# The ramp of the first feed-forward reordered: first unit's norm first, weights scaled in two parts, filler products on TensorE

## The reference

```python
x = x + 0.5 * ffn(layernorm(x))
x = x + attn(layernorm(x), Q, K, VO)      # 16 heads, rank 64
x = x + 0.5 * ffn(layernorm(x))

def ffn(x):                                # three blocks
    h = x
    for blk in range(3):
        y = qlora_linear(h, 2*blk)         # w = (q/7.5 - 1)*scale, + bias, + lora_b @ lora_a
        y = gelu(layernorm(y) * gamma + beta)
        h = qlora_linear(y, 2*blk+1) + h
    return h
```

## Time and profile before

| | us |
|---|---|
| median of 3 runs | 995.24 (993.47 to 997.75) |
| profiled execution: its own time | 993.64 |
| profiled execution: span, first to last instruction | 991.8 |
| TensorE busy | 956.4 (96%) |
| VectorE busy | 853.0 (86%) |
| ScalarE busy | 809.2 (82%) |
| GpSimd busy | 831.7 (84%) |

### The profile page before, as it was taken

How to read it: one execution, slowest core, us unless ns; L and a number is a source line. 1 busy time by engine, 2 the same in 40 slices (tenths; PEclk the granted TensorE clock), 3 DMA queues, 4 the chain that set the end, 5 groups by cost and what they waited for, 6 DMA issues and landing times.

```text
span 991.8 us, 19434 instructions
## 1 busy us (share of the span) xinstructions
PE 956.4 (96%) x6005; PEld 509.0 (51%) x6005; DVE 853.0 (86%) x1731; ACT 809.2 (82%) x1344; POOL 831.7 (84%) x940
## 2 busy tenths in 40 slices
PE   4889799999999999999999999999999999999898
PEld 4677344444444444444444444444444444445677
DVE  7678899999999999999999999999999988995554
ACT  3876689888888898888888888888888888888773
POOL 3655599999998999899999999999999998899552
PEclk9999999999999999999999999999999999999999
DMA  9000322222222222222222222222222222220002
GB/s 252 1 2 11 86 65 64 65 64 65 64 62 58 64 64 56 67 63 62 61 61 63 65 64 65 64 65 64 64 65 64 65 64 55 69 62 10 1 1 86
DMA packets 71744, 59.89 MB, mean 60 GB/s; under 512 B 11168, under 2 KB 70560, under 8 KB 71648
## 3 DMA queue, kind: packets, MB, share of 16 engines
q1 hardware_dynamic: 71392, 58.31, 23.3%
q10 hardware_dynamic: 256, 0.39, 0.1%
HBM read 6.23 MB, written 2.10 MB: 8 GB/s over the span
## 4 chain that ended last, share of the span: by engine, by line
PE 90%; DVE 5%; POOL 2%; issue 1%; DMA 1%; ACT 1%; SPq 0%; POOLq 0%; DVEq 0%; ACTq 0%
PE ps L1194 12%; PE ps L1186 11%; PE ps L1196 11%; PE ps L1195 11%; PE ps L1187 11%; PE ps L1179 7%; PE ps L1170 3%; PE ps L1213 3%; PE ps L1209 3%; PE ps L1210 3%; PE ps L1092 3%; PE ps L1172 3%; PE ps L1171 3%; PE ps L1121 2%; PE ps L1102 1%; PE ps L1133 1%
## 5 line engine op out<-in xcount | busy, mean ns | idle before, releaser
L469 POOL TENSOR_TENSOR p_lo<-work_b,p_hi 128x1024 f16<-128x1024 f32 x256 | 540.0, 2131 | 48.2 <-ACT p_hi L620 47.6
L923 DVE TENSOR_REDUCE mcol<-ps 128x2 f16<-128x1024 f32 x256 | 301.2, 1221 | 3.5 <-PE ps L1179 3.4
L615 ACT ACTIVATE work_b<-ps,exp_scale 128x1024 f32<-128x1024 f32 x256 | 271.5, 1111 | 35.2 <-PE ps L1187 34.6
L620 ACT ACTIVATE p_hi<-work_b 128x1024 f16<-128x1024 f32 x256 | 256.1, 1055 | 0.0
L1194 PE MATMUL ps<-p_hi,xn_hi 128*128 128x512 f16 x512 | 194.7, 380 | 1.2 <-DVE pair_ops L912 1.2
L1186 PE MATMUL ps<-head_ops 128*128 128x512 f16 x512 | 194.1, 379 | 1.8 <-DVE head_ops L934 1.4
L1195 PE MATMUL ps<-p_hi,xn_lo 128*128 128x512 f16 x512 | 194.0, 379 | 0.0
L1196 PE MATMUL ps<-p_lo,xn_hi 128*128 128x512 f16 x512 | 194.0, 379 | 0.0
L1187 PE MATMUL ps<-head_ops 128*128 128x512 f16 x512 | 194.0, 379 | 0.0
L478 POOL TENSOR_TENSOR x<-x,o_sb 128x512 f32<-128x512 f32 x128 | 162.8, 1272 | 7.5 <-DVE o_sb L951 2.1
L934 DVE STREAM_TRANSPOSE head_ops<-mcol 32x128 f16<-32x128 f16 x512 | 155.4, 304 | 9.3
(11 more groups left out here) (135 smaller groups left out, 1375.2 us busy)
## 6 DMA issues: line engine op xcount, KB each, us to landing
head_ops<-pair_ops SPq DMA_DIRECT2D x512, 64.0 KB, 2.0
head_ops<-pair_ops SPq DMA_DIRECT2D x128, 128.0 KB, 2.4
x<-x_dram SPq DMA_DIRECT2D x8, 256.0 KB, 5.9
out<-x SPq DMA_DIRECT2D x8, 256.0 KB, 2.3
vo_last<-wvo_dram SPq DMA_DIRECT2D x1, 1024.0 KB, 12.2
qk<-wq_dram SPq DMA_DIRECT2D x1, 512.0 KB, 5.3
qk<-wk_dram SPq DMA_DIRECT2D x1, 512.0 KB, 6.1
scl<-scales_dram ACTq DMA_DIRECT2D x8, 48.0 KB, 5.0
```

What stands on the lines that cost most here:

```text
L469: pool.tensor_tensor(p_lo[:, k % 2, rows, :], p32[:, k % 2, rows, :], p_hi[:, k % 2, rows, :], ALU.subtract).then_inc(plo_done, 1)
L615: nc.scalar.activation(p32[:, k % 2, 2 * a:2 * a + 2, :], s_ps[a], ACT.Exp, scale=exp_scale[:, 0:1]).then_inc(exp_done, 1)
L620: nc.scalar.activation(p_hi[:, k % 2, 2 * a:2 * a + 2, :], p32[:, k % 2, 2 * a:2 * a + 2, :], ACT.Copy).then_inc(phi_done, 1)
L923: nc.vector.tensor_reduce(mcol[:, pair % 2, :, t, 0], max_ps[pair == 1][t % 2], AX.X, ALU.max, negate=True).then_inc(max_red, 1)
```

## The change

Four things in the first feed-forward's ramp; the second feed-forward and attention keep their order.

1. The norm is done unit by unit: batches 0 and 1, then 2 and 3, then 4 to 7 (three rounds of the 1/sigma chain). ScalarE makes batch 2's sums itself (`input_sums`). VectorE normalizes batches 0, 2, 4, 6, 7, ScalarE 1, 3, 5. VectorE does unit 0's seed, and z_scaled(0, 0), between the statistics.
2. Weights 0 and 1 are loaded and made first; weights 2 to 5 are dequantized and scaled by POOL (`scale_weights`) into `w_rest`, their LoRA part is copied by ScalarE, and VectorE adds and centres them in step 3 (`w_ready`, on which TensorE waits in step 4).
3. TensorE issues filler products (`keep_warm(10)`) twice; turns and products go unit by unit, and lin2(0, 0) stands ahead of pre(2).
4. POOL's clears of `head_ops` for the fourth operand go into steps 4 to 6; the load of ScalarE's Gelu table moves to the start.

```diff
 @block.sync
             for b in range(SG):
                 load_x(b)
-            sp.dma_start(qw[:, :, :], qw_d).then_inc(w_in, 16)
...
+            for g in range(G // 2, G):
+                load_scales(sp, g, slice(0, 2), w_first_in)
             for b in range(SG, B):
                 load_x(b)
+            sp.dma_start(qw[:, 2:NL, :], qw_d[:, 2:NL, :]).then_inc(w_rest_in, 16)
+            for g in range(G):
+                load_scales(sp, g, slice(2, NL), w_rest_in)
+            sp.dma_start(gam[:, :], gam_d).then_inc(gb_in, 16)
+            sp.dma_start(bet[:, :], bet_d).then_inc(gb_in, 16)
 @block.gpsimd
-            pool.wait_ge(prep_p, 5)
-            pool.memset(head_ops[64:128, :, 3, :], 0.0).then_inc(prep_p, 1)
-            pool.wait_ge(prep_p, 6)
-            pool.memset(head_ops[64:65, 0:2, 3, :], 1.0).then_inc(prep_p, 1)
-            pool.memset(head_ops[64:65, 2:RING, 3, :], 1.0).then_inc(prep_p, 1)
...
+            def scale_weights(dst, layers):
+                plink(pool, pool.tensor_scalar(dst, qw[:, layers, :], 1.0 / 7.5, -1.0, ALU.mult, ALU.add))
+                return pool.tensor_tensor(dst, dst, scl[:, layers, :], ALU.mult)
+
+            def clear_heads(part):
+                pool.wait_ge(rstd_ready, part + 5)
+                if part == 0:
+                    pool.memset(head_ops[64:128, :, 3, :], 0.0).then_inc(prep_p, 1)
+                else:
+                    pool.memset(head_ops[64:65, 2 * part - 2:2 * part, 3, :], 1.0).then_inc(prep_p, 1)
+                pool.wait_ge(prep_p, 6 + part)
+
+            pool.wait_ge(prep_p, 5)
             for i in range(STEPS):
                 newton(0, i)
                 if i == 0:
+                    pool.wait_ge(w_rest_in, 16 * (G + 1))
+                    scale_weights(w_rest[:, :, :], slice(2, NL)).then_inc(rest_scaled, 1)
                     pool.wait_ge(a_in, 16 * 4)
                 if i < H // 4:
                     fold_last(4 * i)
                     fold_last(4 * i + 2)
+                if i in (4, 5, 6):
+                    clear_heads(i - 4)
 @block.scalar
+            act.dma_start(bias[:, :], bias_d).then_inc(bias_in, 16)
+            act.dma_start(la[:, :, :], la_d).then_inc(lora_in, 16)
+            act.dma_start(lb[:, :, :], lb_d).then_inc(lora_in, 16)
+            act.dma_start(qw[:, 0:2, :], qw_d[:, 0:2, :]).then_inc(w_first_in, 16)
+            for g in range(G // 2):
+                load_scales(act, g, slice(0, 2), w_first_in)
             act.wait_ge(consts, 2)
+            nc.scalar.activation(gelu_warm[:, :], mean_mat[:, 0:1], ACT.Gelu)
...
+            def input_sums(b):
+
+                act.wait_ge(x_in[b], 16)
+                for t in range(TT):
+                    cols = slice(t * D, (t + 1) * D)
+                    ins = nc.scalar.activation(work_b[:, b, cols], x[:, b * TT + t, :], ACT.Identity, scale=1.0 / D,
+                                               accum_out=mv[:, b * TT + t, 0:1])
+                ins.then_inc(sums_done, 1)
+                act.wait_ge(sums_done, 1)
+                for t in range(TT):
+                    cols = slice(t * D, (t + 1) * D)
+                    ins = nc.scalar.activation(work_b[:, b, cols], x[:, b * TT + t, :], ACT.Square, scale=-1.0,
+                                               bias=mv[:, b * TT + t, 0:1], accum_out=mv[:, b * TT + t, 1:2])
+                ins.then_inc(sums_done, 1)
+
+            input_sums(2)
+            act.wait_ge(prep_pe, 2)
+            nc.scalar.activation(wt[:, 2:NL, :].rearrange("p n d -> p (n d)"), lora_rest, ACT.Copy).then_inc(lora_copied, 1)
...
+            act.wait_ge(moments_ready, 1)
+            norm_apply(1)
+            pre(0)
+            pre(1)
+            squares(0, 0)
+            act.wait_ge(moments_ready, 2)
+            norm_apply(3)
+            pre(2)
+            pre(3)
+            squares(0, 1)
+            act.wait_ge(moments_ready, 3)
+            norm_apply(5)
+            act.wait_ge(gb_in, 32)
+            gelu(0, 0)
+            pre(4)
+            pre(5)
+            squares(0, 2)
+            pre(6)
+            pre(7)
+            squares(0, 3)
+            for i in range(4, STEPS):
+                gelu(0, i - 3)
                 squares(0, i)
-                if i == 1:
-                    norm_apply(1)
-                    pre(1)
                 weight_halves(i)
 @block.vector
+            input_stats([0])
+            split_bias()
+            input_stats([1])
+            norm_means(batch_tiles(0, 2))
+            norm_sigmas(batch_tiles(0, 2))
+            norm_apply(batch_tiles(0))
+            dve.wait_ge(w_first_in, 16 * (G + 1))
+            link(dve, nc.vector.tensor_scalar(wt[:, 0:2, :], qw[:, 0:2, :], 1.0 / 7.5, -1.0, ALU.mult, ALU.add))
+            link(dve, nc.vector.tensor_tensor(wt[:, 0:2, :], wt[:, 0:2, :], scl[:, 0:2, :], ALU.mult))
             dve.wait_ge(prep_pe, 1)
...
+            centre(0, 1).then_inc(prep_v, 1)
+            input_stats([3])
+            norm_means(batch_tiles(3))
+            dve.wait_ge(sums_done, 2)
+            norm_sigmas(batch_tiles(2, 2), batch_tiles(2))
...
-            norm_input(1)
-            for i in range(STEPS):
+            seed(0, 0)
+            norm_apply(batch_tiles(2))
+            input_stats([4, 5, 6])
+            z_scaled(0, 0)
+            input_stats([7])
+            seed(0, 1)
+            norm_means(batch_tiles(SG, SG))
+            norm_sigmas(batch_tiles(SG, SG))
+            norm_apply(batch_tiles(4))
+            norm_apply(batch_tiles(6))
+            norm_apply(batch_tiles(7))
+            for i in range(2, STEPS):
+                if i == 3:
+                    dve.wait_ge(rest_scaled, 1)
+                    dve.wait_ge(lora_copied, 1)
+                    link(dve, nc.vector.tensor_tensor(wt[:, 2:NL, :], wt[:, 2:NL, :], w_rest[:, :, :], ALU.add))
+                    centre(2, NL).then_inc(w_ready, 1)
 @block.tensor
+            nc.tensor.matmul(bmean_ps, mean_mat[:, :], bias[:, :], start=True, stop=True).then_inc(bmean_done, 1)
...
+            def keep_warm(count):
+
+                for n in range(count):
+                    nc.tensor.matmul(warm_ps, mean_mat[:, :], mean_mat[:, :], start=True, stop=True)
+
+            keep_warm(10)
...
             pre(0)
-            turn_bias()
             pe.wait_ge(prep_v, 1)
             pe.wait_ge(bias_ready, 1)
-            for i in range(STEPS):
+            lin1(0, 0)
+            keep_warm(10)
+            pre(1)
+            lin1(0, 1)
+            turn_z(0, 0)
+            lin2(0, 0)
+            pre(2)
+            lin1(0, 2)
+            pre(3)
+            lin1(0, 3)
+            turn_z(0, 1)
+            for i in range(4, STEPS):
+                if i == 4:
+                    pe.wait_ge(w_ready, 1)
                 lin1(0, i)
-                if i == 1:
-                    pre(1)
...
```

More of the change, by code:

```diff
@@ L287, in at, with load_scales @@
             return (f * STEPS + i) * 2 + c + 1
+        def load_scales(eng, g, layers, done):
+            rows = 128 // G
+            eng.dma_start(scl[rows * g:rows * g + rows, layers, :],
+                          sc_d[g][layers, :].partition_broadcast(rows)).then_inc(done, 16)
         class Link:
@@ L528, in apply_half, with norm_apply @@
                 ins.then_inc(done, 1)
[L530 to L537, removed]
+            def norm_apply(b):
+                for t in range(b * TT, (b + 1) * TT):
+                    ins = nc.scalar.activation(xhat[:, t, :], x[:, t, :], ACT.Identity, scale=rstd[:, t:t + 1],
+                                               bias=shift[:, t:t + 1])
+                ins.then_inc(xhat_a, 1)
             def squares(f, i):
@@ L714, in _, with rsqrt @@
             link = Link()
-            def rsqrt(tiles):
+            def rsqrt(tiles, summed):
                 v, y, r, u = var[:, tiles], rstd[:, tiles], rs_t[:, tiles], rs_u[:, tiles]
-                link(dve, nc.vector.tensor_scalar(v, mv[:, tiles, 1], LN_EPS, None, ALU.add))
+                if summed is not None:
+                    nc.vector.tensor_scalar(var[:, summed], mv[:, summed, 1], 1.0 / D, LN_EPS, ALU.mult, ALU.add)
+                    plain = slice(summed.stop, tiles.stop)
+                else:
+                    plain = tiles
+                link(dve, nc.vector.tensor_scalar(var[:, plain], mv[:, plain, 1], LN_EPS, None, ALU.add))
                 link(dve, nc.vector.tensor_scalar(y.bitcast(I32), v.bitcast(I32), -0.5, MAGIC, ALU.mult, ALU.add))
@@ L818, in _, with input_stats @@
-            link(dve, nc.vector.tensor_reduce(wmean[:, :], wt[:, :, :], AX.X, ALU.add))
-            link(dve, nc.vector.tensor_scalar(wmean[:, :], wmean[:, :], -1.0 / D, None, ALU.mult))
-            for n in range(0, NL, 2):
-                ins = nc.vector.tensor_scalar(wt[:, n, :], wt[:, n, :], wmean[:, n:n + 1], None, ALU.add)
-            ins.then_inc(prep_v, 1)
+            def input_stats(batches):
+                for b in batches:
```

(11 more changed lines are left out.)

145 lines of the change are left out of this document (63 added, 82 removed).

## The result

The changed kernel takes 1002.15 us (median of 6, 1001.55 to 1004.33) against 995.37 (median of 6) of the kernel before: ratio 1.0073, 95% interval 1.006 to 1.0086. It is slower by 6.8 us. The forecast was 998.9, 4.5 above its base. A second measurement of the same kernel, described with the experiments, gave 1.0061 (1.0044 to 1.0079).

The account below looks back on a forecast made before the run. TensorE, busy 96% of the span, bounds the kernel, so the date it passes turn_tops decides. Later turn_tops +1.4 and slow pace +3.1 give +4.5 on a base of 994.4: 998.9 us, range 993.5 to 1002.5.

Parts of the forecast that it names:

- The middle, where the gain goes: Ramp from prep_v to turn_tops: moments_ready 3 1.1 later, TensorE standing 7.0 us, lin1(0,4) 2.3 later, turn_tops 1.4 later.
- B: TensorE at the gap ahead of lin2(0,0): pace stays fast, +1.4, 995.8 us; chance 0.24.
- D: Start on TensorE: filler products do not bring the pace, +9, 1003 us or more; chance 0.07.
- E: Norm of units 2 and 3 is not last; the start's 5.6 us carry through, less caps: -4, 990.4; chance 0.06.
- rival C: As forecast, but input_sums, first weights' loads slip and slow pace fills lin1(0,2): +6.5 to +7, 1001; chance 0.18.
- Costs nothing: POOL's clears moved into steps 4 to 6: newton(0,5) ends at 57.5, its z needed at 64.1; no cost.
- Slow pace, coming back within lin1(0,2): TensorE after standing 7.0 us: lin2(0,0), turns and part of lin1(0,2) at slow pace, +3.1.
- Nobody waits for it: keep_warm(10) fillers on TensorE: done between 12.3 and 14.5, no delay, as batch 1's xhat comes at 13.8.
- 1.4 forecast without the pace: Ramp's end at turn_tops: 57.0 against 55.57, counting order and waits without slow pace.

Follow-up runs that it names:

- VectorE's order: Changed kernel with norm_apply(2) and batch 4's stats ahead of seed(0,0), postponed weights and weight_maxima(0) ahead of seed(0,2) on VectorE: 997.54 us, 1.0024.
- the norm first: Combined-edits kernel (991.92 us) with batches 4 to 7's norm ahead of seed(0,1) and z_scaled(0,0), turn_z(0,0), lin2(0,0) and gelu(0,0) later: 990.6 us, 0.995.
- the moves at turn_tops: Changed kernel with weight_maxima(2) ahead of z_scaled(0,4) and turn_tops behind lin2(0,3): 1001.55 us, 1.0068.
- all edits together: Changed kernel with 30 fillers in the gap, clears at the start, folds later, maximum and turn_tops moved; lin2(0,0) stays ahead of unit 2: 997.35 us, 1.0027.

## Why the prediction was right or wrong

Right: the direction, and the mechanism up to lin2(0,0) and its slow pace. "The middle, where the gain goes" holds in each step: the start came 5.3 sooner (5.6 forecast), seed(0,0) at 18.52 (18.0), TensorE stood 7.7 us (7.0) ahead of lin2(0,0), released by Gelu behind norm_apply(5), and came out of it at half pace. lin1(0,4) followed 5.8 after the start of seed(0,2) (5.5 forecast). Rivals B, D and E are out: the pace fell, the fillers brought it (1.05 for the first eight, without them 1.91), nothing carried through. The measured 1002.15 lies at the upper edge of the range, where rival C stood, but not by C's mechanism: input_sums took 2.9 us, less than the 3.9 taken, no load of the first weights was late, and the pace was back before lin1(0,2).

Wrong: the size, 6.8 against 4.5, and with it the weight of the chances: I gave 0.66 to a change of under 0.5% and 0.30 to a slower kernel, and it is 0.7% slower. Three terms of the sum failed.

"Costs nothing" for the moved clears, and nothing for the folds. I followed POOL's work for when its results are needed, and not for what lies beside it on VectorE. POOL's first fold waited for vo_last until 28.25 (27 forecast), which put it beside the third chain. The folds cost 1.0 there (4.73 against 3.78 with the folds moved), and half a microsecond on L876 (0.98 for two at 45.20 beside a fold, 0.48 in the kernel of VectorE's order), the clear 0.75 ahead of turn_tops (2.37 against 1.63 with the clears moved). The Trainium skill, "SBUF — State Buffer", in the section on who interferes with whom, says that VectorE and GpSimd share a pair of ports which is locked for a whole instruction, and that the loser waits in full. By that rule a small instruction ends when POOL's does, and the traces agree (29.69 with 29.66, 59.15 with 59.12).

"Slow pace, coming back within lin1(0,2)" was taken as one stretch worth 3.1. It was worth less, 2.2 (11.49 against 9.32), as the pace came back during the turns of batches 4 and 5. But there were three stretches, 5.4 together; that the first was taken too dear hides 0.9 of the miss. The second follows 2.0 us of standing ahead of lin1(0,4) in six of the eight profiles that have this gap; it costs 1.65 in the profile after (lin1(0,4) to lin2(0,1) in 3.85 instead of 2.2). The third, behind turn_tops, costs 1.55 (4.25 against 2.70) in one profile of the changed kernel and nothing in the other. I had bounded the cost of standing by the gap of 2.57 in the kernel before, which kept its pace, and so held gaps of 2 us free. The same trace has the 2.45 us at 929.43, also without a fall; both were draws, as the other profiles show. The rule weighed in the prediction (the Trainium skill, "TensorE: Matmul & The Clock Gate", its part on the clock gate: an idle stretch brings the throttled state back) agrees with the first stretch, granted clock 0.50 from 32 to 34, and I didn't ask it about the shorter gaps. The row of 2.57 is one case, no bound: 2.0 us were followed by half pace here, 3.22 us in the kernel without fillers were not.

The dates ahead of the third chain were late: lin1(0,0) by 0.3, seed(0,0) by 0.5, seed(0,1) by 0.6. "Nobody waits for it" of the fillers was wrong: they ended at 13.55, both batches of unit 0 were normalized at 13.12, and their turns began only behind the fillers; in other profiles these ended up to 0.6 later.

The sum of the corrected terms, against the profile: 1.4 forecast without the pace, +0.5, +1.0 and +0.75 for the dates and POOL, 2.2 + 1.65 + 1.55 for the pace: 9.05 of 9.2, with differences of 0.3 either way left in the middle.

The medians are 6.8 apart because the profile before is a low draw, and because stretches of half pace come in some executions and not in others. Every timed execution comes with its span and mean granted clock. Of 65 executions of the kernel before, measured beside the experiments, 14 have a clock of 1.00 and spans of 991.6 to 992.8, 34 have 0.996 to 0.998 (991.6 to 994.0), and 17 have 0.993 to 0.995 (994.0 to 996.3). So the kernel before loses pace too in many executions. Of the twelve of the changed kernel eleven have 0.990 to 0.995, and one 0.997. How often the third stretch comes, these means don't tell: both profiles of the changed kernel have 0.993, with it and without it.

Where the loss goes by experiment, in steps from the changed kernel (1.0067, mean of its two measurements): VectorE's order -4.3, lin2(0,0) behind unit 2 -2.2, folds -1.1, clears -1.2, pace in the first gap -0.8 by time and 2.2 in the trace, turn_tops nothing by time. Only VectorE's order is clear of the intervals of both measurements of the changed kernel, and lin2(0,0) behind unit 2 of one; the folds, the clears and the pace rest on their traces. The steps overlap, since the edits that close a gap also take the slow stretch behind it; together with the norm first they give -11.7.

Open: why fillers in the gap and the moves at turn_tops, both seen in their traces, hardly show in the medians; and what decides whether a gap of 2 to 3 us is followed by half pace. The order of instructions alone doesn't, as the 2.45 us of the second feed-forward show.

## What to carry to other kernels

A sooner start is worth nothing if the same order lets an in-order queue wait for a later norm with other units' work behind it; follow the date at which the steady stream begins, not the first product, and put work without a deadline into the engine's waits, not between a seed and the step that releases TensorE. When work is moved on POOL, price it by what VectorE does beside it, even if nobody waits for its result. In these runs standings of TensorE from 2.0 us up were often followed by half pace for 1.5 to 2.2 us of loss, so closing a gap can be worth more than its length. One profile without a fall doesn't show that a gap is free.

## What the runs showed of the hardware

- Half pace after standing: lin2(0,0) at 3.78 instead of 1.98 after 6.8 to 7.8 us of standing, in all seven profiles that have the gap unfilled ahead of lin2(0,0). With unit 2 ahead of it, the eight turns behind 6.38 us took 1.97. After 2.0 us of standing lin1(0,4) had half pace in six profiles, and in two not (no fillers, and all edits together). 2.37 us ahead of turn_tops were followed by it in two profiles and not in two, 3.21 us in one, 3.22 us not in one. The 2.45 us ahead of the second feed-forward's first lin2, the same in all fourteen profiles, were followed by it in four.
- Instructions on VectorE of 0.17 to 0.18 took up to 1.76 beside a memset or a tensor_tensor of POOL and ended with it: TENSOR_SCALAR and COPY beside a memset, TENSOR_SCALAR, SCALAR_TENSOR_TENSOR and TENSOR_TENSOR beside a tensor_tensor. The statistics kept their 0.87 for four beside the clears.
- The granted clock reads 1.00 at the start of each trace although the products there have half the pace; it shows half only from the first fall on.
